# Second expert products of two mixture layers: one 512-column stream for both halves of the weights instead of two of 256

## The reference, cut to what matters

```python
# layer 0, for each of 32 experts: xe (640, 256), w1, w3, w2 (256, 256)
h = silu(xe @ w1) * (xe @ w3)
out = (h @ w2) * buf_w                 # second product
# layer 1, for each of 8 experts: exp_in (1024, 256), W1 (256, 1024), W2 (1024, 256)
hmid = gelu(exp_in @ W1 + b1)
exp_out = hmid @ W2 + b2               # second product
moe = zeros.at[token].add(exp_out * gate)
```

## Time and profile before

| | |
|---|---|
| median of 3 runs | 1537.81 us (1537.18 to 1538.5) |
| profiled execution: span, first to last instruction | 1506.1 us |
| profiled execution: its own time | not recorded; the median is 31.7 us above the span |
| busy: TensorE, weight loads, VectorE, ScalarE, GpSimd | 92%, 81%, 69%, 60%, 48% |
| layer 0's experts, 176 to 551 us | TensorE busy 363.6 of 375 us |
| layer 1's experts, 1120 to 1494 us | TensorE busy 373.4 of 374 us |

### The profile page before, as it was taken

One profiled execution on the slowest core, in us unless ns is written; L12 is line 12 of the kernel. 1 busy time (PEld: TensorE's weight loads), 2 busy tenths in 40 slices (PEclk: granted clock), 3 DMA queues, 4 the chain that ended last, 5 costly groups with the idle time before them and its releaser, 6 DMA issues.

```text
span 1506.1 us, 27545 instructions
## 1 busy us (share of the span) xinstructions
PE 1392.1 (92%) x9777; PEld 1218.8 (81%) x9777; DVE 1032.3 (69%) x2455; ACT 906.7 (60%) x2160; POOL 719.4 (48%) x712
## 2 busy tenths in 40 slices
PE   7997799999999999779999999999749999999996
PEld 5776799999999998557777778777529899999996
DVE  2999577777777776668887888886535656556552
ACT  5886455555555553257887888878635646546452
POOL 0678543434434324554556666654443535435433
PEclk9988999999999999999999999999959999999998
DMA  5421256566656644456757758666531433324212
GB/s 173 137 90 38 60 155 170 170 170 173 182 168 179 180 112 125 89 94 112 155 107 124 152 108 141 134 115 101 142 99 36 101 96 96 74 63 104 38 21 29
DMA packets 134329, 173.62 MB, mean 115 GB/s; under 512 B 21461, under 2 KB 106272, under 8 KB 134192
## 3 DMA queue, kind: packets, MB, share of 16 engines
q1 hardware_dynamic: 106032, 119.89, 31.1%
q0 software_dynamic: 28160, 51.96, 17.4%
HBM read 107.28 MB, written 42.08 MB: 99 GB/s over the span
## 4 chain that ended last, share of the span: by engine, by line
PE 67%; DMA 11%; DVE 10%; issue 5%; POOL 3%; ACT 3%; SPq 1%; POOLq 0%; DVEq 0%; ACTq 0%
PE banks L948 42%; DMA xe<-pooled,idx 7%; PE banks L1499 4%; PE banks L1456 4%; DMA got<-done,slot 3%; PE banks L1010 3%; PE banks L451 3%; PE banks L1552 2%; DVE X L1719 2%; PE banks L1473 1%; PE banks L1512 1%; POOL table L1448 1%; PE banks L1566 1%; PE banks L1928 1%; PE banks L1471 1%
## 5 line engine op out<-in xcount | busy, mean ns | idle before, releaser
L948 PE MATMUL banks<-hi_x,hi_w 128*128 128x320 f32 (+1 forms) x832 | 288.7, 347 | 10.5 <-DVE hidden L983 5.3
L948 PE MATMUL banks<-lo_x,hi_w 128*128 128x320 f32 (+1 forms) x832 | 286.6, 344 | 0.0
L948 PE MATMUL banks<-hi_x,lo_w 128*128 128x320 f32 (+1 forms) x832 | 286.4, 344 | 0.0
L889 POOL DMA_INDIRECT xe<-pooled,idx x160 | 158.0, 987 | 224.7 <-DVE hidden L983 104.6
L948 PE MATMUL banks<-hi_w,hi_h 128*128 128x256 f32 x896 | 260.5, 291 | 2.4 <-DVE X L1037 2.0
L948 PE MATMUL banks<-hi_w,lo_h 128*128 128x256 f32 x896 | 253.5, 283 | 0.0
L948 PE MATMUL banks<-lo_w,hi_h 128*128 128x256 f32 x896 | 253.4, 283 | 0.0
L1913 POOL DMA_INDIRECT out<-X,tab x64 | 106.3, 1662 | 190.6 <-DVE X L2016 176.0
L1603 ACT ACTIVATE PN<-banks,smax 128x256 f32<-128x256 f32 (+1 forms) x512 | 180.3, 444 | 25.1 <-DVE smax L1709 25.1
L1429 POOL DMA_INDIRECT got<-done,slot x128 | 125.6, 981 | 144.8 <-DVE smax L1709 82.5
L948 PEld LDWEIGHTS banks<-hi_x,hi_w 128*128 128x128 f32 x832 | 159.0, 191 | 24.9 <-issue 10.1
(11 more groups left out here) (189 smaller groups left out, 3038.4 us busy)
## 6 DMA issues: line engine op xcount, KB each, us to landing
w<-in_L_ffn_w SPq DMA_DIRECT2D x96, 256.0 KB, 5.6
done<-res SPq DMA_DIRECT2D x32, 640.0 KB, 3.4
BIG<-in_L_ffn_W SPq DMA_DIRECT2D x16, 1024.0 KB, 9.1
QS<-parts_qk SPq DMA_DIRECT2D x96, 128.0 KB
KS<-parts_qk SPq DMA_DIRECT2D x96, 128.0 KB
mask<-in_c_masks SPq DMA_DIRECT2D x16, 257.0 KB, 2.7
pooled<-XF SPq DMA_DIRECT2D x16, 256.0 KB, 3.2
WS<-in_L_cond_W SPq DMA_DIRECT2D x16, 256.0 KB
```

What stands on the lines that cost most here:

```text
L889: e.indirect_dma_start(xe[:, n % NXE, i, :], None, pooled, bass.IndirectOffsetOnAxis(ap=idx0[:, n * NS0 + i:n * NS0 + i + 1], axis=0)).the ...
L948: last = e.matmul(o, a[i], b[j], start=start and k == 0, stop=stop and k == 2, skip_group_check=True)
```

## The change

- The high and low halves of the weights of both layers lie in one tensor (`parts_w`, `parts_w1`). In a routed expert's second product, one matmul streams both (256 + 256 = 512 columns) against `hi_h` into the two halves of a bank, and one of 256 columns adds `lo_h` by `hi_w` to the first half. Two matmuls take the place of three. The shared expert stays as it was.
- A row tile then fills a bank, so that the two halves must be added when they are read. Layer 0: 5 `down` units per expert instead of 3, on the same two banks; ScalarE copies the first half to `res`, VectorE adds the second to it, and only this frees the bank. Units 0 and 1 come before `turn_xe` 2, units 2 to 4 behind it.
- Layer 1: `down` goes tile by tile (4 steps, all 8 slices of features in each) on banks 5, 6 and 7 in turn. VectorE adds bias, adds the second half, and multiplies by the gate, 256 columns each; each tile's scatter is issued when it is ready.
- The numbers in the hand-written first steps of attention move by the added steps. Two small loads of layer 1 count on another semaphore.

```diff
     def down_pairs(pt):
-        return 2 if shared(pt) else 3
+    def down_units(pt):
+        return 2 if shared(pt) else NS0
...
-            if pt > NSH:
-                yield "down", (pt - 1, 0)
+            first = 0 if pt == NSH else 1 if shared(pt - 1) else 2
+            for u in range(first):
+                yield "down", (pt - 1, u)
             if turning:
                 yield "turn_xe", (parts[nxt][0] - 1, 2)
             if pt > NSH:
-                for u in range(1, down_pairs(pt - 1)):
+                for u in range(first, down_units(pt - 1)):
                     yield "down", (pt - 1, u)
...
+    def pe_wide_product(e, bank, a, b, start, stop):
+
+        e.matmul(PS[:, bank, :], a[0], b, start=start, stop=False, skip_group_check=True)
+        return e.matmul(PS[:, bank, 0:D], a[1], b[:, 0, :], start=False, stop=stop, skip_group_check=True)
...
             for hc in range(2):
+                last = pe_wide_product(e, bank, [t[:, pt % 2, hc, u * P:(u + 1) * P] for t in (hi_h, lo_h)],
+                                       parts_w[j % 2][:, :, 2, hc, :], hc == 0, hc == 1)
         last.then_inc(s_down, 1)
 
+    def act_down(e, pt, u):
+        if shared(pt):
+            return
+        n = parts[pt][0] - 1
+        e.wait_ge(s_down, down_at[pt, u] + 1)
+        if n >= 2 and u == 0:
+            e.wait_ge(s_res_out[n % 2], 16 * (n // 2))
+        e.activation(res[:, n % 2, u, :], PS[:, down_bank(pt, u), 0:D], ACT.Copy).then_inc(s_down_high, 1)
+
     def dve_down(e, pt, u):
...
-            e.tensor_copy(res[:, n % 2, 2 * u:2 * u + w, :],
-                          PS[:, bank, 0:w * D].rearrange("p (a n) -> p a n", n=D)).then_inc(s_down_out, 1)
+            e.wait_ge(s_down_high, NS0 * n + u + 1)
+            e.tensor_tensor(res[:, n % 2, u, :], res[:, n % 2, u, :], PS[:, bank, D:2 * D], ALU.add).then_inc(s_down_out, 1)
...
+    def down1_bank(u, i):
+
+        return 5 + (NS1 * u + i) % 3
...
-            elif step == "down" and d == 0:
+            elif step == "down":
+                if NS1 * u + d >= 3:
+                    e.wait_ge(s_biased, 2 * (NS1 * u + d - 2))
                 for f in range(FC):
...
+                    if d == 0:
+                        e.wait_ge(s_h1_lo, FC * u + f + 1)
+                    col = DC * F1 + f * D
+                    last = pe_wide_product(e, down1_bank(u, d), [t[:, f, d * P:(d + 1) * P] for t in (hi_h1, lo_h1)],
+                                           parts_w1[:, :, n % 2, col:col + D], f == 0, f == FC - 1)
+                last.then_inc(s_d1_ps, 1)
...
+                e.tensor_tensor(o, PS[:, bank, 0:D], b2s[:, n % 2, :], ALU.add).then_inc(s_biased, 1)
+                e.wait_ge(s_biased, 2 * (NS1 * u + d) + 1)
+                e.tensor_tensor(o, o, PS[:, bank, D:2 * D], ALU.add).then_inc(s_biased, 1)
+                e.wait_ge(s_biased, 2 * (NS1 * u + d) + 2)
+                e.tensor_scalar(o, o, tab[:, n, h * NS1 + d, 1:2], None, ALU.mult).then_inc(s_weighed, 1)
```

More of the change, by code:

```diff
@@ L332, in _build @@
     w0 = sb("w0", [P, NW0, 3, DC * D], scope=layer0)
-    hi_w, lo_w, hi_x, lo_x = [], [], [], []
+    parts_w, hi_w, lo_w, hi_x, lo_x = [], [], [], [], []
     for i in range(2):
-        for tiles, name, shape in ((hi_w, "hi_w", (3, DC, D)), (lo_w, "lo_w", (3, DC, D)),
-                                   (hi_x, "hi_x", (DC * CAP0,)), (lo_x, "lo_x", (DC * CAP0,))):
-            tiles.append(sb(f"{name}_{i}", [P, *shape], F32R, layer0))
+        parts_w.append(sb(f"parts_w_{i}", [P, 2, 3, DC, D], F32R, layer0))
+        hi_w.append(parts_w[i][:, 0, :, :, :])
+        lo_w.append(parts_w[i][:, 1, :, :, :])
+        for tiles, name in ((hi_x, "hi_x"), (lo_x, "lo_x")):
+            tiles.append(sb(f"{name}_{i}", [P, DC * CAP0], F32R, layer0))
     hi_h, lo_h = (sb(n, [P, 2, 2, CAP0], F32R, layer0) for n in ("hi_h", "lo_h"))
@@ L793, in _build @@
     for pt_ in range(NPT):
-        for u_ in range(down_pairs(pt_)):
+        for u_ in range(down_units(pt_)):
             down_at[pt_, u_] = len(down_at)
@@ L1024, in pe_down @@
         bank = down_bank(pt, u)
-        for i in tiles:
+        if shared(pt):
+            for i in range(2 * u, 2 * u + 2):
+                for hc in range(2):
+                    last = pe_product(e, PS[:, bank, (i % 2) * D:(i % 2 + 1) * D],
+                                      [t[:, pt % 2, hc, i * P:(i + 1) * P] for t in (hi_h, lo_h)],
+                                      [t[j % 2][:, 2, hc, :] for t in (hi_w, lo_w)], hc == 0, hc == 1)
+        else:
             for hc in range(2):
-                last = pe_product(e, PS[:, bank, (i % 2) * D:(i % 2 + 1) * D],
-                                  [t[:, pt % 2, hc, i * P:(i + 1) * P] for t in (hi_h, lo_h)],
-                                  [t[j % 2][:, 2, hc, :] for t in (hi_w, lo_w)], hc == 0, hc == 1)
+                last = pe_wide_product(e, bank, [t[:, pt % 2, hc, u * P:(u + 1) * P] for t in (hi_h, lo_h)],
+                                       parts_w[j % 2][:, :, 2, hc, :], hc == 0, hc == 1)
         last.then_inc(s_down, 1)
+    def act_down(e, pt, u):
+        if shared(pt):
+            return
[4 more added lines that the diff above has]
+        e.activation(res[:, n % 2, u, :], PS[:, down_bank(pt, u), 0:D], ACT.Copy).then_inc(s_down_high, 1)
     def dve_down(e, pt, u):
-        j, bank, w = parts[pt][0], down_bank(pt, u), len(down_tiles(pt, u))
+        j, bank = parts[pt][0], down_bank(pt, u)
         e.wait_ge(s_down, down_at[pt, u] + 1)
@@ L1048, in tail_steps @@
     def tail_steps(*kinds):
-        return [(step, a) for step, a in steps0[tail_begin:] if step in kinds]
+        return [(step, a) for step, a in steps0[tail_begin:]
+                if step in kinds or step == "down" and not shared(a[0])]
     def pe_step0(e, step, a):
@@ L1853, in experts1_order @@
                 yield "load", u + 2, None
-            for q in range(2):
-                yield "down", u, q
+            for i in range(NS1):
+                yield "down", u, i
             if h == NH - 1 and n + 2 < E1:
@@ L1943, in pe_experts1 @@
                 last.then_inc(s_u1_ps, 1)
-            elif step == "down" and d == 0:
+            elif step == "down":
+                if NS1 * u + d >= 3:
+                    e.wait_ge(s_biased, 2 * (NS1 * u + d - 2))
                 for f in range(FC):
-                    e.wait_ge(s_h1_lo, FC * u + f + 1)
-                    for i in range(NS1):
-                        col = DC * F1 + f * D
-                        end = f == FC - 1 and i % 2 == 1
-                        last = pe_product(e, PS[:, 5 + i // 2, (i % 2) * D:(i % 2 + 1) * D],
-                                          [t[:, f, i * P:(i + 1) * P] for t in (hi_h1, lo_h1)],
-                                          [t[:, n % 2, col:col + D] for t in (hi_w1, lo_w1)], f == 0 and i % 2 == 0, end)
-                        if end:
-                            last.then_inc(s_d1_ps, 1)
+                    if d == 0:
[4 more added lines that the diff above has]
+                last.then_inc(s_d1_ps, 1)
     def act_experts1(e):
```

72 lines of the change are left out of this document (31 added, 41 removed).

## The result

The changed kernel takes **1578.5 us** (1576.15 to 1581.69, four runs) against 1537.5 us before in the same measurement (1536.46 to 1538.5, four runs): ratio 1.0256 [1.0233, 1.028], 41.0 us slower. The prediction was 1570.3 (+32.5) in a range of 1549 to 1583, slower with 0.91.

The account below looks back on a forecast made before the run. It took layer 0 as bound by two nearly equal loops, TensorE's own and down copy to gather to turn, and layer 1 by TensorE. Layer 0 +42 and layer 1 -9.5 gave +32.5, 1570.3 us, range 1549 to 1583.

Parts of the forecast that it names:

- What the matmuls save: Both layers: two matmuls for three save one fixed cost, 13 ns a product; 4.2 us and 6.8 us, 11.0 together.
- The way out of a bank: Layer 0's down units: emptying takes 1.14 us against a unit of 0.69, so units 2 and 4 wait 0.64 and 0.45.
- TensorE's loop: Layer 0's iteration when TensorE alone sets the pace: grows by 1.03 us, from 11.73 to 12.76.
- The sum over 29 iterations: Layer 0, experts 2 to 31: 15 iterations of 13.86, five of 13.35, nine of 12.76; 389.5 against 350.93, +38.6 us.
- The gathers give way: Rival, chance 0.25: layer 0's gathers shorten under thinner traffic and TensorE's own iteration sets the pace; +13.5 us, 1551.
- The queues pile up: Rival, chance 0.12: each ScalarE and VectorE hand-over 0.2 us slower than counted, +17 us more, about 1586.
- the matmuls decide: Rival, chance 0.07: layer 0's banks are free when TensorE comes, so layer 0 gains 4 us; -13.5 in all, 1524.
- Layer 1's end: Only the last tile's scatter remains after the last matmul, issued 2.25 us after the stream's end instead of 6.92: -4.7.
- Layer 1's units: Layer 1's 16 units: -6.8 us from the matmuls and +2 from the last slice's wait, -4.8 together.
- the late slice: Layer 1's tile 0 waits for the last slice's low half, 0.1 to 0.2 us in some 14 of 16 units; 2 us.
- The offset: Whole kernel: the median of the runs lies 31.7 us above the profiled span, added to 1538.6 to give 1570.3.

Follow-up runs that it names:

- the later trace of the changed kernel: The changed kernel run once more without an edit, beside the kernel before: 1542.5 us against 1501.8, ratio 1.0278.
- the two runs with an early gather: Fifth gather waiting for the turn instead of the last down copy: in the changed kernel 1522.05 us, in the kernel before 1492.9 us.
- Two tiles side by side: The changed kernel with layer 1's tiles 0 and 1 going through the eight slices together, tiles 2 and 3 one by one: 1540.6 us, ratio 1.0256.
- The parts alone: Layer 0's edits with the old layer 1: 1551.4 us, ratio 1.0339; layer 1's edits with the old layer 0: 1497.7 us, ratio 0.9968.
- layer 1 alone: The change's layer 1 edits with layer 0 as in the kernel before: 1497.7 us, ratio 0.9968.
- one segment: The changed kernel with layer 1's wide matmul reading 512 neighbouring columns instead of two pieces, low halves left out of the sum: 1543.8 us.

## Why the prediction was right or wrong

The direction and the cause were right; the measured time lies in the range, near its upper end, and the forecast of +32.5 was 8.5 too low. By its steps:

- **What the matmuls save**: right where nothing waits. The pair takes 0.346 to 0.347, and the layer 1 without a wait gives 0.39 a unit of the 0.42 counted.
- **The way out of a bank**: right, nearly to the instant. Unit 2 at t = 2.15 (2.24), unit 4 at 4.11 (4.15), out at 6.04 (6.00), gather issued 7.15 after the turn (7.11). TensorE's loop alone 12.75 (12.76). Taking away ScalarE's step and making the gather early each moved the two loops by what they should.
- **The sum over 29 iterations**: right in its form, small in size. +38.6 was predicted, +41.2 measured (13.52 against 13.43). The prediction let the gather set the pace of 20 iterations, 13.73 each in the mean, and TensorE that of nine at 12.76; measured are 23 of 13.71 and six of 12.81. TensorE's loop had grown by 1.03 and the gather's by 1.51, so that a gather is now late when it takes over 12.80 - 7.19 = 5.61 us (11.77 - 5.68 = 6.09 before). In the later trace of the changed kernel just six of the 29 take less, where the prediction had nine. Outside these iterations +4.5 where 3.7 was taken.
- **The gathers give way** (chance 0.25): refuted. In the chains of the changed kernel the fifth gather takes 6.66 and 6.51 in the mean, against 6.71 before, though the traffic fell from 169 to 153 GB/s. The chain picks the late ones; over all whose landing can be read it is 6.2 (29 in the later measurement) against 6.35 (20 of 29 before). For this rival it had to be about 5.5. The prediction's reason, that store, gather and weight loads start together as before and it is they that meet, is borne out by the two runs with an early gather: 3.7 and 3.9.
- **The queues pile up** (0.12) and **the matmuls decide** (0.07): refuted, by the same instants and by the 63 waits.
- **Layer 1's end**: right, -4.7 predicted, 4.7 and 4.8 measured.
- **Layer 1's units**: the term most mis-sized, by 4.1 of the 8.5. -4.8 was predicted (-6.8 for the matmuls, +2 for the late slice). Measured are -0.7. A down phase saves 0.42; the late slice, with the restart, takes about 0.2 back, as high as the prediction had it, and the later pairs, 24 of 0.353 instead of 0.346, take another 0.17 in nearly all phases. The first of the two was known, at 0.1 to 0.2 in 14 units; the second was not. Two tiles side by side remove both, and then the unit takes 22.90.
- **The offset**: 31.7 us between median and span was taken as something that lies around every execution. It isn't: 1.8 us do. The rest was the difference between two executions of the same kernel. That reading was wrong, and only by luck did it no harm: the forecast is the measured median before, 1537.8, plus 32.5, whatever the offset is made of.

With the measured terms the sum is 41.2 + 4.5 - 0.7 - 4.8 = +40.2, and measured are 41.0 and 40.7. The parts alone are +49.2 and -4.5, 44.7 together: the intervals of the ratios, some 4 and 2 us to either side, hold the 4 us of difference.

Open is why pairs are slower after a wait. That they are was seen in the changed kernel, in layer 1 alone and with one segment; where a phase has no wait (the fifteenth unit of these, and 15 units each with tiles side by side) they stay at 0.347. The second segment isn't the cause. But a wait isn't the whole of it: in the later trace of the changed kernel two phases with the same wait, from 1194.92 and from 1264.49, go on at 0.347 and their units take 23.05, and with tiles side by side the last unit's phase runs at 0.354 without a wait in it. Nothing else about it was tried.

## What to carry to other kernels

A product that needs two engines in series to be read has a way out longer than itself; cost that way from end of stream to free bank first (here 1.14 us against a unit of 0.69), and give each unit other work of that length, or another bank, before merging matmuls that save 13 ns each. And read the loops that lie just under the critical one: here the last copy also held a gather, so that a delay of 1.0 us on TensorE cost 1.4 an iteration; one changed wait (the gather behind the turn, not behind the copy) gave 10 us before the change and 20 after it, in part because a gather ahead of the store takes 3.7 to 3.9 us and one behind it 6.2. Work that covers one hand-over may also be covering another: moving the down units away uncovered the turns' splits.

## What the runs showed of the hardware

- Pairs of F32R matmuls of 512 and 256 columns, each with its own weight load, start 0.346 us apart. After one wait for a semaphore in the stream they start 0.353 apart up to the end of the phase, in 15 of the 16 phases of the changed kernel's first trace and in 13 of its later one, in which two more had the wait and stayed at 0.347.
- An indirect gather of 128 rows of 1 KB takes 6.2 us in the mean when it is issued 0.24 us behind a store of 640 KB, and 3.7 when it is issued 2.7 us ahead of it (29 gathers each, the changed kernel once more and the one with its gather early).
- A moving operand in two pieces of 256 columns, one in each half of a tensor, costs the same as 512 neighbouring columns (pairs of 0.353 and units of 23.25 us with either).
- The same program takes 1502 us on three chips and 1537.5 in the first measurement. For the changed kernel, of which there is a trace of either kind, the difference isn't in the experts' stages (13.52 against 13.48 an iteration, 23.25 against 23.22 a unit). From layer 0's last turn to attention it is 66 against 57 us, in attention 424 against 414, and from there to layer 1 110 against 96. The windows of this last stretch, first measurement and then the later one (columns as in the earlier trace rows):

```profile
1080.00:1190.00 110.00, 73.19 (x543) 55.24 (x542) 51.70 (x161) 60.53 (x163) 45.56 (x47) 0.75 0.39 90
```

```profile
1059.00:1155.00 96.00, 63.74 (x550) 49.29 (x548) 52.16 (x164) 60.04 (x164) 45.65 (x47) 0.86 0.51 104
```

The longer one has the lower granted clock (0.75 against 0.86) and the thinner traffic (90 against 104 GB/s) for the same work. Which of them is cause and which effect was not tried, nor what sets the first measurement apart.
